# Adding scaled expert outputs to the residual in DRAM by indirect DMA, and SiLU rewritten with Sigmoid and PSUM operands

## The chip, the cores and the metric

The kernel runs on one core of a Trainium2 chip. The metric is the device time of one execution in microseconds (us); the median of three runs of the kernel before is 1481.43 us, the lowest 1478.41 and the highest 1485.65. Five engines work side by side, each through its own list of instructions: TensorE (PE, with its weight loads as PEld), VectorE (DVE), ScalarE (ACT), GpSimd (POOL) and SyncE (SP). They wait for one another through semaphores. DMAs are issued from SP, POOL and ACT.

## The reference, cut to what matters

The input `x` has 4 sequences of 512 tokens with 256 values each, 2048 tokens in all. Two layers each update `x` twice, and every update is multiplied by the tanh of a gate. The second update of each layer is a mixture of eight experts, of which each token uses its best two. Only the mixtures are touched by the change:

```python
# layer 0 (m=0 in the kernel), F = 256; a shared FFN is added as well
p = softmax(h @ w_router.T); top2 of 8 experts, shares renormalised
y = sum over the two experts e of share[e] * (relu(h @ w1[e].T)**2 @ w2[e].T)
x = x + tanh(g_ffn[0]) * (shared(h) + y)
# layer 1 (m=1), F = 512
y = sum over the two experts e of
      share[e] * ((silu(h @ gate_w[e] + gate_b[e]) * (h @ up_w[e] + up_b[e])) @ down_w[e] + down_b[e])
x = x + tanh(g_ffn[1]) * y
```

## The kernel before, in words

All data is float32. A matmul operand is split into a high part (rounded to the type fp32r, which TensorE takes) and a low part (the rest), and `product` (L194 to L196) makes each product of three matmuls. Activations are split by ACT (the rounding copy) and DVE (a subtraction). Expert weights are split on the way in: `weights_hi` (L438) is a casting DMA issued by POOL, and `weights_lo` (L446) is one POOL `tensor_tensor` that subtracts the high part from `raw`, a plain copy of the weights loaded by SP (L376).

The program has five stretches. Part A (attention, shared FFN and the choice of experts of layer 0) lasts until about 386 us of the span. The expert loop of m=0 runs until 521, part C (slot attention with a recurrent update, and the choice of experts of layer 1) until about 1131, the expert loop of m=1 until 1410, and the rest is the combination of m=1. Orders written out by hand set parts A and C; the expert loops are hardware loops.

**Scattering.** When the experts of a batch of 512 tokens are chosen, POOL issues eight indirect DMAs (L759), each of which writes 128 normalised rows of 256 values to their place in the DRAM tensor `routed[m]`, which is sorted by expert. Each expert's rows are filled up with zero rows to groups of G = 256. A table in SBUF holds the first and the last group of each expert. This input gives 19 groups for m=0 and 21 for m=1.

**The loop.** For each expert, each engine runs a hardware loop over its groups. In one turn SP loads the group after the next into `xg` (L387) and stores the result `y` to the DRAM tensor `outputs` (L426). PE multiplies the group with the up weights (in m=1 the gate and the up weights, four parts `f` of 128 columns), turns the rows of the next group (L543), and multiplies with the down weights. For m=0, ACT makes the relu (L475) and its rounded square (L477), DVE makes h in SBUF (L509) and its low part (L521, L524). For m=1, silu(g)·u is computed as (tanh(g/2)+1)·(g/2)·u: ACT writes the tanh (L480) and g/2 (L481) to SBUF, DVE multiplies these two (L513, both inputs in SBUF), then multiplies with the up part in PSUM (L516) and writes h to SBUF; ACT rounds h (L484, L487) and DVE makes the low part from h and the rounded h (L521, L524, both in SBUF). ACT and DVE also split the turned next group (L466, L497). Last, DVE copies the down product out of PSUM (m=0, L529) or adds the bias `DB` (m=1, L531). There is one buffer for `raw`, `xg` and `y`, and two for the split weights of an expert.

**The weights' order.** POOL holds, for each next expert, `weights_hi` and then at once `weights_lo`, without a loop. SP issues the raw weights between the group loops (`raw_in`), and in m=0 at the third expert also five loads of part C's weights (`attention_weights`, L383).

**The combination.** After the loop, POOL waits for the last store and gathers the two rows of each token from `outputs` with 8 indirect DMAs for each batch (L819; 32 for each m), by row numbers `source` that `table_dve` computes. DVE multiplies each with its share and adds it to the residual, 8 instructions a batch (L1257). The residual had been stored to `x_base` and is loaded again. In m=1 SP stores the sum to `out` (L721).

## Time and profile before

| | us |
|---|---|
| median of three runs (lowest, highest) | 1481.43 (1478.41, 1485.65) |
| span of the profiled execution, first to last instruction | 1462.4 |
| its own device time | not recorded beside the span; the three runs lie 16.0 to 23.3 above it |
| PE busy in the span | 1092.1 (75%) |
| DVE / ACT / POOL busy | 790.0 / 418.9 / 362.7 |
| DMA traffic | 114.66 MB, mean 78 GB/s |
| mean granted TensorE clock | 0.872 of full speed |

Stretch by stretch, busy microseconds of each engine:

| stretch of the span | PE | DVE | ACT | POOL | granted clock | DMA share |
|---|---|---|---|---|---|---|
| 402 to 521 (loop of m=0) | 77.97 | 53.45 | 37.49 | 26.46 | 0.89 | 0.61 |
| 521 to 575 (start of part C) | 26.36 | 27.41 | 17.99 | 26.46 | 0.66 | 0.32 |
| 1148 to 1410 (loop of m=1) | 215.51 | 175.75 | 109.89 | 60.53 | 0.91 | 0.40 |
| 1410 to 1462 (combination of m=1) | 0.00 | 13.37 | 0.00 | 31.05 | 0.52 | 0.53 |

A busy share says how full an engine is and not whether it is waited for; the chain of waits says that. Lines are named by number, L513 is line 513 of the kernel before. SPq is SP's queue of DMA issues.

### The profile page before, as it was taken

Reading aid. Unit: us, or ns where it says so; the run is one execution under the profiler, and the core shown is the slowest. Engines: PE = TensorE matmul, PEld = TensorE weight load, DVE = VectorE, ACT = ScalarE, POOL = GpSimd, SP = SyncE. Lnnn points to the kernel's source line nnn. Section 1 sums busy time; section 2 is a strip of 40 time slices with the busy share of each in tenths; the row PEclk is TensorE's granted clock in tenths of the full one; section 3 lists DMA queues with packets and bytes.
Section 4 is the critical chain, followed back from the end, with each engine's and each line's share of the span. In section 5 each row is a group of like instructions: output and inputs, shape, how many; then the busy total and the mean of one; then the engine's idle time right before and its main releaser. Section 6 shows DMA issues by size and latency. Waiting matters only on the chain.

```text
span 1462.4 us, 16573 instructions
## 1 busy us (share of the span) xinstructions
PE 1092.1 (75%) x5562; PEld 904.4 (62%) x5562; DVE 790.0 (54%) x1774; ACT 418.9 (29%) x788; POOL 362.7 (25%) x294
## 2 busy tenths in 40 slices
PE   1978889787666663998999579898971488897850
PEld 1647666575565662786777458686860377897840
DVE  5456546656444436646565544535455466667633
ACT  1203121122132341233332332424220144453420
POOL 4204152131421351410101220101014322213225
PEclk9989989897888985999999679999985599998985
DMA  7600032000375650200000100000005544443435
GB/s 265 225 1 29 1 119 68 1 0 1 132 212 167 179 174 0 58 0 1 1 0 15 44 29 0 1 0 1 1 1 190 176 130 130 130 137 122 129 99 168
DMA packets 92431, 114.66 MB, mean 78 GB/s; under 512 B 6608, under 2 KB 77776, under 8 KB 92240
## 3 DMA queue, kind: packets, MB, share of 16 engines
q1 hardware_dynamic: 72480, 78.46, 16.5%
q0 software_dynamic: 19888, 35.40, 8.3%
q8 instruction: 34, 0.56, 0.2%
q14 instruction: 29, 0.24, 0.1%
HBM read 77.14 MB, written 36.70 MB: 78 GB/s over the span
## 4 chain that ended last, share of the span: by engine, by line
PE 53%; DVE 22%; issue 6%; POOL 6%; ACT 6%; DMA 5%; SPq 2%; DVEq 0%; POOLq 0%; ACTq 0%
PE PS L194 12%; PE PS L196 11%; PE PS L195 11%; PE PS L1577 7%; PE PS L1493 4%; DVE act L513 3%; PE PS L1468 3%; DMA xg<-routed 3%; POOL routed L759 2%; POOL HB L819 2%; POOL rstd L752 2%; PE PS L1389 1%; PE PS L1516 1%; DVE st L1036 1%; DVE SM L1310 1%
## 5 line engine op out<-in xcount | busy, mean ns | idle before, releaser
L752 POOL TENSOR_TENSOR rstd<-ve,minus_half 128x4 f32<-128x4 f32 x40 | 40.6, 1016 | 410.1 <-DVE ve L1043 251.6
L194 PE MATMUL PS<-xt,split 128*128 128x256 f32 x412 | 121.3, 295 | 10.9 <-issue 7.8
L194 PE MATMUL PS<-split,hs 128*128 128x256 f32 x244 | 84.2, 345 | 49.8 <-DVE hs L521 49.8
L195 PE MATMUL PS<-xt,split 128*128 128x256 f32 x412 | 119.3, 290 | 0.0
L196 PE MATMUL PS<-xt,split 128*128 128x256 f32 x412 | 118.9, 289 | 0.0
L1577 PE MATMUL PS<-VP,HB 128*128 128x257 f32 x384 | 97.0, 416 | 16.0 <-DVE VP L1322 16.0
L1577 PEld LDWEIGHTS PS<-VP,HB 128*128 128x128 f32 x384 | 80.1, 210 | 35.2 <-DVE VP L1322 21.8
L513 DVE SCALAR_TENSOR_TENSOR act<-act 128x256 f32<-128x256 f32 x84 | 70.8, 843 | 56.2 <-ACT act L481 56.2
L446 POOL TENSOR_TENSOR split<-raw,split 128x1024 fp32r<-128x1024 f32 (+1 forms) x15 | 66.5, 4432 | 138.4 <-DMA raw<-down_w 81.9
L194 PEld LDWEIGHTS PS<-xt,split 128*128 128x128 f32 x412 | 82.6, 200 | 14.4 <-issue 10.5
L194 PEld LDWEIGHTS PS<-split,hs 128*128 128x128 f32 x244 | 55.9, 229 | 57.1 <-DVE hs L521 57.1
L759 POOL DMA_INDIRECT routed<-S,dest x64 | 65.6, 1024 | 100.2 <-DVE dest L1114 83.0
L195 PEld LDWEIGHTS PS<-xt,split 128*128 128x128 f32 x412 | 82.3, 200 | 0.0
L196 PEld LDWEIGHTS PS<-xt,split 128*128 128x128 f32 x412 | 81.8, 199 | 0.0
L819 POOL DMA_INDIRECT HB<-outputs,source x64 | 63.3, 990 | 73.0 <-DMA outputs<-y 54.2
L195 PE MATMUL PS<-split,hs 128*128 128x256 f32 x244 | 78.1, 320 | 0.0
L196 PE MATMUL PS<-split,hs 128*128 128x256 f32 x244 | 77.8, 319 | 0.0
L543 PE MATMUL PS<-ident,xg 128*128 128x128 f32 x168 | 28.2, 294 | 56.3 <-DMA xg<-routed 56.3
L480 ACT ACTIVATE act<-PS,hbg 128x256 f32<-128x256 f32 x84 | 39.6, 472 | 94.5 <-PE PS L196 94.5
L1389 PE MATMUL PS<-ident,S 128*128 128x128 f32 x208 | 31.1, 299 | 45.1 <-DVE S L1047 45.1
L981 ACT ACTIVATE HB<-PS,SM 128x512 f32<-128x512 f32 x48 | 33.0, 688 | 107.8 <-DVE SM L1312 107.4
L194 PE MATMUL PS<-HTS,WHH 128*128 128x512 f32 x144 | 60.4, 419 | 2.0 <-DVE RT L1051 2.0
(308 smaller groups left out, 2871.4 us busy)
## 6 DMA issues: line engine op xcount, KB each, us to landing
xg<-routed SPq DMA_DIRECT2D x44, 256.0 KB, 2.7
outputs<-y SPq DMA_DIRECT2D x40, 256.0 KB, 3.0
outputs<-zeros SPq DMA_DIRECT2D x3, 2048.0 KB, 16.1
routed<-zeros SPq DMA_DIRECT2D x20, 256.0 KB, 2.5
raw<-m_w SPq DMA_DIRECT2D x16, 256.0 KB, 5.9
split<-m_w POOLq DMA_DIRECT2D x16, 256.0 KB, 4.0
x_base<-X SPq DMA_DIRECT2D x8, 512.0 KB, 3.8
raw<-gate_w SPq DMA_DIRECT2D x8, 512.0 KB, 6.3
```

The lines of the kernel that those rows point to most:

```text
L194: pe.matmul(out_, a[1], b[0], start=first, stop=False)
L195: pe.matmul(out_, a[0], b[1], start=False, stop=False)
L196: return pe.matmul(out_, a[0], b[0], start=False, stop=last)
L446: eng.tensor_tensor(w.split[e % 2][:, 1], w.raw[:], w.split[e % 2][:, 0].bitcast(F32), ALU.subtract).then_inc(sem(f"m{m}_lo"), 1)
L513: dve.scalar_tensor_tensor(out=a[:, 0], in0=a[:, 0], scalar=1.0, in1=a[:, 1], op0=ALU.add, op1=ALU.mult).then_inc(sem(f"m{m}_silu"), 1)
L752: pool.tensor_tensor(rstd[h][:], ve[h][:], minus_half[:], ALU.pow).then_inc(sem("rstd_ready"), 1)
L759: pool.indirect_dma_start(out=routed[m], out_offset=bass.IndirectOffsetOnAxis(ap=dest[m][:, n, j, kk:kk + 1], axis=0), in_=S2[h][:, j], in ...
L819: pool.indirect_dma_start(out=rows_h[h][:, kk, j], out_offset=None, in_=outputs, in_offset=bass.IndirectOffsetOnAxis(ap=source[:, n, j, kk ...
L1389: ins = pe.transpose(bank(h, k + c)[:, j * P:(j + 1) * P], src[:, j, c * P:(c + 1) * P], ident[:])
L1468: ins = pe.matmul(bank(h, b + c), w[:, j, c * P:(c + 1) * P], EWT[:, j], start=j == 0, stop=j == TT - 1)
L1493: ins = pe.matmul(token_banks(h, 0)[:, j], HB[h][:, m, j * P:(j + 1) * P], W2[:, m], start=m == 0, stop=m == HC - 1)
L1577: ins = pe.matmul(bank(h, j)[:, 0:D + 1], HB[h][:, m, j * P:(j + 1) * P], VP[h][:, m, 0:D + 1], start=m == 0, stop=m == TT - 1)
```

## The change

**Rows that know where they belong.** A row of `routed` is four values wider (W = 260): its token number, the share of its second expert, the difference of the first share to that, and the number of its first expert. The choice of experts writes these into `rows_of`, which the eight scattering DMAs send as before. Rows that fill a group (`pad`) carry a token number past the last token and shares of 0.

**The loop.** In each group ACT copies these values to `meta` (`keep`), DVE makes from them each row's share (`row_scale`) and its row number (`row_number`), and ACT writes `y` times the share with two ACTIVATEs (`y_out`; in m=0 straight from PSUM in place of L529, in m=1 after DVE's bias addition). One turn later POOL copies the row numbers and issues two indirect DMAs of 128 rows with addition (`add_rows`). In m=0 one half of a group is added to `x_base[0]` and the other to a second tensor, `x_add`. In m=1 both halves go to `x_base[1]`, and the second half waits until the first has landed. The store of `y`, the tensor `outputs`, its zero fill of three times 2048 KB (now one, for `x_add`), `source` and all 64 gathers are gone.

**The combination.** In m=0 it is one DVE addition of `x_add` for each batch, which is loaded beside the residual. In m=1 there is none: after the last addition SP copies `x_base[1]` to `out` with four DMAs of 512 KB from DRAM to DRAM.

**The split of expert weights.** POOL now runs the group loop too. `weights_hi` of the next expert stands ahead of an expert's loop, `weights_lo` behind its last turn. The load of `raw` moves from SP to ACT's queue at the start of an expert.

**SiLU.** ACT writes a Sigmoid (one ACTIVATE a part in place of two), DVE multiplies it with the biased gate part read from PSUM, then with the up part, and writes h to PSUM; the high and the low part are made from there. In m=0 h is written to PSUM as well. In m=1 the split of the next group now stands ahead of the low part of the last h.

**Starts.** Five of the eight fills of `routed` are issued by ACT, and the first group is loaded after all eight (before: after three). The five loads of part C's weights are issued by SP right at the start of m=0's loop. A few small operations are added to the choice of experts.

```diff
+        sums = [(x_base[0], x_add), (x_base[1], x_base[1])]
...
         def group_in(sp, m, t):
             r = sp.value_load(table[m][0:1, bass.ds(t + 2 * E, 1)], min_val=0, max_val=XROWS - G)
+            if not isinstance(t, int):
+                counted(sp, m)
+                sp.wait_ge(sem(f"m{m}_turned"), t)
+                sp.wait_ge(sem(f"m{m}_kept"), t)
             sp.dma_start(moe[m].xg[:], routed[m][bass.ds(r, G), :].rearrange("(a p) d -> p a d", p=P)).then_inc(sem(f"m{m}_xg"), 16)
...
+        def moe_sp(sp, m):
             sp.wait_ge(sem(f"m{m}_turned"), 1)
+            sp.wait_ge(sem(f"m{m}_kept"), 1)
             group_in(sp, m, 1)
...
+            if m == 0:
+                attention_weights(sp)
+            else:
+                raw_in(sp, 1, 1)
+            total = sp.value_load(table[m][0:1, 2 * E - 1:2 * E], min_val=1, max_val=NG)
+            with sp.Fori(0, total) as t:
+                group_in(sp, m, t + 2)
+            moe_end(sp, m, total)
...
+            def add_rows(t):
+                pool.wait_ge(sem(f"m{m}_next_row"), t + 1)
+                for a in range(2 - m):
+                    pool.wait_ge(sem(f"m{m}_yout{a}"), 16 * (1 + m) * t + 16)
+                pool.sem_inc(sem("passed"), 1)
+                pool.tensor_copy(to_row[:], next_row[:]).then_inc(sem(f"m{m}_to_row"), 1)
+                pool.wait_ge(sem(f"m{m}_to_row"), t + 1)
+                for a in range(G // P):
+                    pool.wait_ge(sem(f"m{m}_y"), 2 * t + 1 + a)
+                    if m == 1 and a == 1:
+                        pool.wait_ge(sem("m1_yout0"), 32 * t + 32)
+                    pool.sem_inc(sem("passed"), 1)
+                    pool.indirect_dma_start(out=sums[m][a], out_offset=bass.IndirectOffsetOnAxis(ap=to_row[:, a:a + 1], axis=0),
+                                            in_=w.y[:, a], in_offset=None, compute_op=ALU.add).then_inc(sem(f"m{m}_yout{a - a * m}"), 16)
+            for a in range(2 - m):
+                pool.dma_start(sums[m][a][B * T:B * T + P], pad[:, 0:D]).then_inc(sem(f"m{m}_yout{a}"), 16)
             pool.wait_ge(sem(f"m{m}_table"), 1)
-            for e in range(2, E):
-                if m == 0 and e == 3:
+            for h in two:
+                pool.wait_ge(sem(f"x_out{h}"), 16 * PAIRS * (m + 1))
+            for e in range(E):
+                if m == 0 and e == 2:
                     attention_weights_hi(pool)
-                weights_hi(pool, m, e)
-                weights_lo(pool, m, e)
+                if 1 <= e < E - 1:
+                    weights_hi(pool, m, e + 1)
+                lo, hi = bounds(pool, m, e)
+                with pool.Fori(lo, hi) as t:
+                    counted(pool, m)
+                    add_rows(t)
+                if 1 <= e < E - 1:
+                    weights_lo(pool, m, e + 1)
+            counted(pool, m)
+            add_rows(hi)
+            moe_end(pool, m, hi)
...
+            def h_hi(t, f):
+                act.wait_ge(sem(f"m{m}_h"), t * w.fc + f + 1)
+                act.activation(w.hs[:, 0, f], h_part(f), ACT.Copy).then_inc(sem(f"m{m}_hhi"), 1)
+            def keep(n):
+                act.wait_ge(sem(f"m{m}_xg"), 16 * n)
+                if not isinstance(n, int):
+                    act.wait_ge(sem(f"m{m}_next_row"), n)
+                    act.wait_ge(sem(f"m{m}_scale"), 2 * n - 2)
+                act.activation(meta[:], w.xg[:, :, D:W], ACT.Copy).then_inc(sem(f"m{m}_kept"), 1)
+            def y_out(t):
+                act.wait_ge(sem(f"m{m}_scale"), 2 * t + 2)
+                if m == 0:
+                    act.wait_ge(sem(f"m{m}_down"), t + 1)
+                else:
+                    act.wait_ge(sem(f"m{m}_biased"), t + 2)
+                for a in range(G // P):
+                    if m == 0:
+                        act.wait_ge(sem(f"m{m}_yout{a}"), 16 * t + 32)
+                    act.activation(w.y[:, a], PS[:, 5 + a, 0:D] if m == 0 else w.y[:, a], ACT.Copy,
+                                   scale=scale[:, a:a + 1]).then_inc(sem(f"m{m}_y"), 1)
...
-                            act.activation(w.act[:, f % 2, 0], PS[:, f, 0:G], ACT.Tanh, bias=hbg[:, b:b + 1], scale=0.5)
-                            act.activation(w.act[:, f % 2, 1], PS[:, f, 0:G], ACT.Identity, bias=hbg[:, b:b + 1], scale=0.5).then_inc(sem(f"m{m}_act"), 1)
+                            act.activation(w.act[:, f % 2, 0], PS[:, f, 0:G], ACT.Sigmoid, bias=col("gate_b", b)).then_inc(sem(f"m{m}_act"), 1)
                             if f:
-                                act.wait_ge(sem(f"m{m}_h"), t * w.fc + f)
-                                act.activation(w.hs[:, 0, f - 1], w.h[:, f - 1], ACT.Copy).then_inc(sem(f"m{m}_hhi"), 1)
-                    if m == 1:
-                        act.wait_ge(sem(f"m{m}_h"), t * w.fc + w.fc)
-                        act.activation(w.hs[:, 0, w.fc - 1], w.h[:, w.fc - 1], ACT.Copy).then_inc(sem(f"m{m}_hhi"), 1)
-                    x_hi(t + 2)
+                                h_hi(t, f - 1)
+                    if m == 0:
+                        keep(t + 2)
+                        x_hi(t + 2)
+                    else:
+                        x_hi(t + 2)
+                        h_hi(t, w.fc - 1)
+                        keep(t + 2)
+                    y_out(t)
...
+            def h_lo(t, f):
+                dve.wait_ge(sem(f"m{m}_h"), t * w.fc + f + 1)
+                dve.wait_ge(sem(f"m{m}_hhi"), t * w.fc + f + 1)
+                dve.tensor_tensor(w.hs[:, 1, f], h_part(f), w.hs[:, 0, f].bitcast(F32), ALU.subtract).then_inc(sem(f"m{m}_hlo"), 1)
+            def row_scale(t, e):
+                dve.wait_ge(sem(f"m{m}_kept"), t + 1)
+                dve.scalar_tensor_tensor(out=here[:], in0=meta[:, :, E0 - D], scalar=float(e), in1=meta[:, :, DSH - D],
+                                         op0=ALU.is_equal, op1=ALU.mult).then_inc(sem(f"m{m}_scale"), 1)
+                dve.wait_ge(sem(f"m{m}_scale"), 2 * t + 1)
+                dve.wait_ge(sem(f"m{m}_y"), 2 * t + 2)
+                dve.tensor_tensor(scale[:], here[:], meta[:, :, SH1 - D], ALU.add).then_inc(sem(f"m{m}_scale"), 1)
+            def row_number(t):
+                dve.wait_ge(sem(f"m{m}_to_row"), t + 1)
+                dve.tensor_copy(next_row[:], meta[:, :, TOK - D]).then_inc(sem(f"m{m}_next_row"), 1)
...
-                            dve.scalar_tensor_tensor(out=a[:, 0], in0=a[:, 0], scalar=1.0, in1=a[:, 1],
-                                                     op0=ALU.add, op1=ALU.mult).then_inc(sem(f"m{m}_silu"), 1)
+                            dve.scalar_tensor_tensor(out=a[:, 1], in0=PS[:, f, 0:G], scalar=col("gate_b", e * w.fc + f),
+                                                     in1=a[:, 0], op0=ALU.add, op1=ALU.mult).then_inc(sem(f"m{m}_silu"), 1)
                             dve.wait_ge(sem(f"m{m}_silu"), t * w.fc + f + 1)
-                            dve.scalar_tensor_tensor(out=w.h[:, f], in0=PS[:, f, G:2 * G], scalar=col("up_b", e * w.fc + f),
-                                                     in1=a[:, 0], op0=ALU.add, op1=ALU.mult).then_inc(sem(f"m{m}_h"), 1)
+                            dve.scalar_tensor_tensor(out=h_part(f), in0=PS[:, f, G:2 * G], scalar=col("up_b", e * w.fc + f),
+                                                     in1=a[:, 1], op0=ALU.add, op1=ALU.mult).then_inc(sem(f"m{m}_h"), 1)
                         if f:
-                            dve.wait_ge(sem(f"m{m}_h"), t * w.fc + f)
-                            dve.wait_ge(sem(f"m{m}_hhi"), t * w.fc + f)
-                            dve.tensor_tensor(w.hs[:, 1, f - 1], w.h[:, f - 1], w.hs[:, 0, f - 1].bitcast(F32), ALU.subtract).then_inc(sem(f"m{m}_hlo"), 1)
-                    dve.wait_ge(sem(f"m{m}_h"), t * w.fc + w.fc)
-                    dve.wait_ge(sem(f"m{m}_hhi"), t * w.fc + w.fc)
-                    dve.tensor_tensor(w.hs[:, 1, w.fc - 1], w.h[:, w.fc - 1], w.hs[:, 0, w.fc - 1].bitcast(F32), ALU.subtract).then_inc(sem(f"m{m}_hlo"), 1)
-                    x_lo(t + 2)
-                    dve.wait_ge(sem(f"m{m}_down"), t + 1)
-                    dve.wait_ge(sem(f"m{m}_yout"), 16 * t + 1)
+                            h_lo(t, f - 1)
                     if m == 0:
-                        dve.tensor_copy(w.y[:], PS[:, 5:7, 0:D]).then_inc(sem(f"m{m}_y"), 1)
+                        h_lo(t, w.fc - 1)
+                        x_lo(t + 2)
                     else:
+                        x_lo(t + 2)
+                        h_lo(t, w.fc - 1)
+                        row_number(t)
+                        dve.wait_ge(sem(f"m{m}_down"), t + 1)
+                        dve.wait_ge(sem(f"m{m}_yout0"), 32 * t + 48)
                         dve.tensor_tensor(w.y[:], PS[:, 5:7, 0:D], DB[:, e].unsqueeze(1).to_broadcast([P, G // P, D]),
-                                          ALU.add).then_inc(sem(f"m{m}_y"), 1)
+                                          ALU.add).then_inc(sem(f"m{m}_biased"), 1)
...
-            def combine(m, n, h):
-                x_t = residual(n, h) if m == 0 else X[h]
...
+            def combine(n, h):
+                if n < 2:
+                    dve.wait_ge(sem(f"x_in{h}"), 16 * (PAIRS + 2))
                 else:
-                    dve.wait_ge(sem(f"x_in{h}"), 16 * (PAIRS + 1) + (m and 16 * (n // 2 + 1)))
...
-                    for j in range(TT):
-                        ins = dve.scalar_tensor_tensor(out=x_t[:, j], in0=rows_h[h][:, kk, j], scalar=share[m][:, n, j, kk:kk + 1],
-                                                       in1=x_t[:, j], op0=ALU.mult, op1=ALU.add)
...
+                    dve.wait_ge(sem(f"second_in{h}"), 48)
+                x_t = residual(n, h)
+                dve.tensor_tensor(x_t[:], x_t[:], added[n], ALU.add).then_inc(sem("combined"), 1)
...
+            for n in range(B):
+                sp.dma_start(out[n], x_base[1][n * T:(n + 1) * T]).then_inc(sem(f"x_out{n % 2}"), 16)
```

On POOL, in the loop of m=1, this stood for one next expert (L438 `weights_hi`, L446 `weights_lo`, L434 reads the table):

```order
L434 TENSOR_LOAD table
L434 ISA x2
L438 DMA split<-gate_w 128x2x512
L438 DMA split<-up_w 128x2x512
L438 DMA split<-down_w 128x4x256
L446 TENSOR_TENSOR split<-raw,split 128x3072
```

and this stands there now for one expert (L442 and L450 are the two halves of the split, L466 and L473 are `add_rows`):

```order
L487 UNCONDITIONAL_BRANCH
L462 REGISTER_ALU
L464 ISA
L466 COPY to_row<-next_row 128x2
L469 ISA
L473 DMA x_base<-y,to_row 2176x256
L469 REGISTER_ALU
L471 REGISTER_ALU
L473 DMA x_base<-y,to_row 2176x256
L487 REGISTER_ALU
L487 COMPARE_AND_BRANCH
L450 TENSOR_TENSOR split<-raw,split 128x3072
```

The subtraction moved behind the additions of the expert's last group turn, and each turn holds two DMAs that were not on POOL.

On DVE, the end of one turn of the loop of m=1 was this (parts 2 and 3 of h, then the split of the next group and the bias):

```order
L505 REGISTER_ALU
L513 SCALAR_TENSOR_TENSOR act<-act 128x256
L516 SCALAR_TENSOR_TENSOR h<-PS,colv,act 128x256
L521 TENSOR_TENSOR hs<-h,hs 128x256
L524 TENSOR_TENSOR hs<-h,hs 128x256
L496 REGISTER_ALU
L497 TENSOR_TENSOR xt<-PS,xt 128x512
L526 REGISTER_ALU
L527 ISA
L531 TENSOR_TENSOR y<-PS,DB 128x512
```

and is now this (L603 and L606 are the two multiplications, L569 the low part of h, L562 that of the next group, L583 `row_number`):

```order
L595 REGISTER_ALU
L603 SCALAR_TENSOR_TENSOR act<-PS,colv,act 128x256
L606 SCALAR_TENSOR_TENSOR PS<-PS,colv,act 128x256
L569 TENSOR_TENSOR hs<-PS,hs 128x256
L561 REGISTER_ALU
L562 TENSOR_TENSOR xt<-PS,xt 128x512
L569 TENSOR_TENSOR hs<-PS,hs 128x256
L583 CAST next_row<-meta 128x2
L618 ISA
L619 TENSOR_TENSOR y<-PS,DB 128x512
```

Every large operation now names PS among its inputs, the split of the next group stands one place earlier, and the row numbers stand ahead of the bias.

On SP, between and in the group loops of m=0, this stood (L376 raw weights, L387 the next group; the store of y, L426, follows):

```order
L376 DMA raw<-m_w 128x2x256 x2
L354 TENSOR_LOAD table
L354 ISA x2
L355 TENSOR_LOAD table
L355 ISA x2
L420 UNCONDITIONAL_BRANCH
L422 REGISTER_ALU
L386 ISA
L386 TENSOR_LOAD table
L386 ISA x2
L387 ISA
L387 DMA xg<-routed 128x2x256
```

and this stands there now:

```order
L429 UNCONDITIONAL_BRANCH
L429 ISA
L399 TENSOR_LOAD table
L399 ISA x2
L402 REGISTER_ALU
L404 ISA
L404 DMA xg<-routed 128x2x260
L429 REGISTER_ALU
L429 COMPARE_AND_BRANCH
```

The raw weights no longer stand ahead of a group's load, and no store of y follows it.

## Rows read from the trace of the kernel before

**Rows 1.** Page, the chain that ended last: shares of the span by engine.

```profile
PE 53%; DVE 22%; issue 6%; POOL 6%; ACT 6%; DMA 5%; SPq 2%; DVEq 0%; POOLq 0%; ACTq 0%
```

**Rows 2.** Chain of waits in m=1's loop: start us, us, what.

```profile
1159.53 6.39 DVE hs L521
...
1194.43 6.90 DVE act L513
...
1366.20 5.99 DVE act L513
```

**Rows 3.** Groups by line, 1150 to 1410: count, busy us, mean ns, idle us.

```profile
L513 DVE SCALAR_TENSOR_TENSOR act<-act 128x256 f32<-128x256 f32 x84 | 70.8, 843 | 56.2 <-ACT act L481 56.2
L484 ACT ACTIVATE hs<-h 128x256 fp32r<-128x256 f32 x63 | 26.2, 416 | 32.9 <-DVE h L516 32.6
```

**Rows 4.** Timeline, POOL and DVE, m=1: start us, us, instruction, [idle before].

```profile
1158.69 6.93 POOL L446 TENSOR_TENSOR split<-raw,split 128x3072 fp32r<-128x3072 f32 x1 [17.94 <-DMA raw<-down_w]
1159.13 0.48 DVE L516 SCALAR_TENSOR_TENSOR h<-PS,colv,act 128x256 f32<-128x256 f32 x1
1194.34 6.70 POOL L446 TENSOR_TENSOR split<-raw,split 128x3072 fp32r<-128x3072 f32 x1 [11.71 <-DMA raw<-down_w]
```

**Rows 5.** SP's timeline in m=1: stores of y, the first, three, the last.

```profile
1171.24 0.39 SPq L426 DMA_DIRECT2D outputs<-y  x1
...
1191.71 0.39 SPq L426 DMA_DIRECT2D outputs<-y  x1
...
1208.77 0.39 SPq L426 DMA_DIRECT2D outputs<-y  x1
...
1218.44 0.39 SPq L426 DMA_DIRECT2D outputs<-y  x1
...
1409.59 0.39 SPq L426 DMA_DIRECT2D outputs<-y  x1
```

**Rows 6.** Timelines of DVE and POOL in the tail.

```profile
1408.63 0.69 DVE L531 TENSOR_TENSOR y<-PS,DB 128x512 f32<-128x512 f32 x1 [0.56 <-PE PS L196]
1412.68 1.04 POOL L819 DMA_INDIRECT HB<-outputs,source  x1 [40.77 <-DMA outputs<-y]
...
1452.22 0.95 POOL L819 DMA_INDIRECT HB<-outputs,source  x1 [0.30 <-issue]
```

**Rows 7.** DMA issues: count, KB each, median us from issue to landing.

```profile
outputs<-zeros SPq DMA_DIRECT2D x3, 2048.0 KB, 16.1
...
out<-X SPq DMA_DIRECT2D x4, 512.0 KB, 3.3
...
routed<-S,dest POOLq DMA_INDIRECT x64, 2.4
HB<-outputs,source POOLq DMA_INDIRECT x64, 2.8
```

**Rows 8.** The gathers' line L819: us from issue to landing.

```profile
DMA to landing us min/median/max: 2.6/2.8/6.8
```

**Rows 9.** SP's timeline, m=0.

```profile
410.32 0.40 SPq L426 DMA_DIRECT2D outputs<-y  x1
...
475.86 1.00 SPq L376 DMA_DIRECT2D raw<-m_w  x2
479.30 0.38 SPq L387 DMA_DIRECT2D xg<-routed  x1
...
516.19 0.39 SPq L426 DMA_DIRECT2D outputs<-y  x1
...
520.58 0.39 SPq L426 DMA_DIRECT2D outputs<-y  x1
```

**Rows 10.** PE's transposes of xg in m=0, 405 to 521: idle us, times.

```profile
  DMA xg<-routed: 25.6, 8
```

**Rows 11.** DVE's timeline at the start of part C.

```profile
544.72 8.06 DVE L1291 TENSOR_TENSOR KK<-S,KK 128x1024 fp32r<-128x1024 f32 x1 [4.42 <-ACT KK L963]
552.70 3.37 DVE L1257 SCALAR_TENSOR_TENSOR X<-HB,share,X 128x256 f32<-128x256 f32 x8
```

232 lines of the change are left out of this document (94 added, 138 removed), and 4 rows, old and new, of the table ORDER_C.

## The prediction, made before the changed kernel was run

> **What bounds the kernel now.** I began with the page's chain that ended last: 53% of it is PE and 22% DVE [rows 1]. So the kernel is not bound by DMA or POOL as a whole, and an edit pays only where the chain leaves PE. The chain read in order of time shows two such places that this change touches. In the loop of m=1 single DVE operations of 6 to 7 us stand in the chain; there are seven, one on L521 and six on L513 [rows 2]. All 84 of L513 take 70.8 us; without the six, at 6.3, 33 are left for 78, 0.42 each [rows 3]. The timeline shows why: POOL's split of an expert's weights, L446, starts at 1194.34 and lasts 6.70 us, and the long L513 starts at 1194.43 and ends with it [rows 2, 4]. L513 and L521 read two tiles in SBUF. An operation that reads one from PSUM is not stretched: L516 began at 1159.13, inside the split that began at 1158.69, and took its usual 0.48 [rows 4].
>
> What a split costs a group is read from SP's stores of y. Without one they are 9.67 us apart (1208.77 to 1218.44), with one 17.06 (1191.71 to 1208.77). From the first to the last store 20 intervals take 238.35 us [rows 5]. Twenty of 9.67 are 193.4, so 45 is over. About 1 us at each of six steps into a new expert stays (an estimate: the seven long operations lie between 5.9 and 6.9, less 0.42, so the six splits in these intervals make 36 to 39). I put the six at 39. The seventh falls in group 0 and costs up to 6.0 ahead of the first store.
>
> The other place is the tail. The last bias addition ends at 1409.32 and the span at 1462.4, 53.1 us later; 32 gathers of about 1.28 us fill 40 of these, one behind another [rows 6].
>
> **Durations that the trace lacks.** No DMA with addition is in it. I call L the time from its issue to its landing, for 128 rows of 1 KB. The indirect write of 128 such rows has a median of 2.4, the indirect read 2.8 [rows 7], the read's worst is 6.8 [rows 8]. An addition has to read and to write, so I take 3.6 (2.4 with 1.2 for the reading, half of 2.4), with the ends 2.4 and 6.8. The Trainium skill, "DMA: Bandwidth & Descriptors", fits a DMA issued by GpSimd with 2.0 us and bytes over 436 GB/s, which would be 2.3 for 128 KB, close to the 2.4 of [rows 7]. With L = 2.3 the sum below would be some 22 us lower; that is a rival further down.
>
> The four copies from DRAM to DRAM are not in it either. Stores of 512 KB take 3.3 each, so 13 in a row; the three zero fills have a median of 16.1, in which 4 MB were written, so 8 for 2 MB [rows 7]. A copy reads as well: 16 and 2 to land make the upper end. I take 12, between 8 and 18.
>
> **Tail: 53.1 before.** Now: the first half of `y_out` 0.42 (as L484, [rows 3]) and 0.3 for POOL to start; the first addition 3.6, the second, which waits for it, 3.6 and 0.1; the wait's release and SP's issues 0.8; the copies 12. Sum 20.8, gain 32. Ends: 8 and L = 2.4 give 14.4 (gain 39), 18 and L = 6.8 give 33.2 (gain 20).
>
> **Loop of m=1.** Two things happen to the six splits. The stretched DVE operations go, since L603, L606 and L569 each read PSUM, as L516 did unhindered [rows 4]. But the split now stands behind the additions of the expert's last turn. What stands behind the waiting POOL instruction is the split itself, and PE waits for it before the next expert. Count from the end of a down product: 0.56 and 0.69 to the end of the bias [rows 6], 0.42 for `y_out`, 0.1, L = 3.6, 1.04 for the second issue [rows 6], 6.7 for the split [rows 4], 0.3 to PE: 13.4. The group's own work is 9.7, so PE waits 3.7 at each of six experts, 22 us. Before it was 39: gain 17. Group 0 is relieved of up to 6.0; against it stands loading ACT's table for the Sigmoid, which I put at 2, for a gain of 4. Small operations are added: per group `keep`, `row_scale`, `row_number` and two ACTIVATEs, about 1.5 us over ACT and DVE. ACT and DVE are idle at the start of a group (L513 waited 56.2 us in all for ACT, which waited for PE, [rows 3]), so I put them at 0.2 a group, 4 us. The Sigmoid form saves an ACTIVATE in each part, which shortens the last part's path by about 0.4 a group, at most 8; cover for it is PE's transposes and the first three down weights, so I take nothing. Together gain 17. Ends: L = 2.4 and all of the 8, gain 33; the whole gain of the splits lost, 0.
>
> The buffer y is a loop of its own now: bias 0.69, `y_out` 0.42, 0.3, two additions one behind another 2L. That is 1.4 + 2L = 8.6 at L = 3.6, just under 9.67. It takes over from L = 4.15.
>
> The port rule bears on `row_scale` (two small SBUF inputs) and `row_number` (a copy). The Trainium skill, "SBUF — State Buffer", section "Who interferes with whom", says that such operations contend with GpSimd and that the second one waits until the first is done; the 6.90 of [rows 2] agrees for two inputs, and no row has such a copy. By it `row_number` would hold the bias of the expert's last group until the split ends. At L = 3.6 this costs nothing, as PE waits for the same split; at L = 5 it would add about 2 us at each of six experts.
>
> **Loop of m=0.** The stores of 19 groups go from 410.32 to 520.58: 18 intervals of 6.13 on average; an undisturbed one is 4.39 (516.19 to 520.58) [rows 9]. PE waits 25.6 us for xg in 8 cases [rows 10], and the order shows one reason: two loads of raw weights stand ahead of the group's load, which follows 3.4 us later (475.86, 479.30 [rows 9]). With raw on ACT's queue I let 16 of the 25.6 go. Against it, POOL's turn is a loop: both additions landed, copy of the numbers 0.4, first issue and gap 1.35, second addition L: 1.75 + L = 5.35. That is over 4.39, by 0.96 in about ten undisturbed turns: 10 lost. Net gain 6. The five loads of part C's weights are now early, beside the first groups; that I leave in the range. Ends: gain 18 (L = 2.4, no turn held), loss 15 at L = 4.5.
>
> **Start of part C.** L1291 took 8.06 at 544.72, beside POOL's weight subtractions. Scaled from L1257 (3.37 for 8 times 256 columns [rows 11]) its 1024 columns are worth 1.7. Without gathers these subtractions run some 20 us earlier, when DVE waits for PE: gain 6.4. The combination of batches 0 and 1 is one addition of 1024 columns each, 1.7 for 3.37: gain 3.4. Instead of a store's 3.0 the last group needs `y_out`, two issues and L, about 5.6: loss 2.5. The extra loads of `x_add` lie beside other loads. With 1 us for the later batches the gain is 8; ends 12 and, if the loads are late by one of 512 KB, 3.
>
> **Starts of the loops.** All eight fills come before the first group's load, but five go through another queue: loss 2 in m=0, gain 2 in m=1. The additions to the choice of experts lose 1.
>
> **Sum.** −32 −17 −6 −8 +1 = −62. The span would be 1400.4. The median of the runs is 19.0 over the profiled span of 1462.4 and I carry that over: 1419.4, which I round to 1420.
>
> **Rivals.** (A) The split gives back all that the ports gave. For this the split's late place, and ACT, which issues the raw loads only when the weights before are split, speak: the split of a two-group expert may then find its raw weights not landed. At 6.5 a step in place of 3.7 the gain of 17 is gone: 1437. Against it, raw is asked for a whole expert ahead. (B) The slower side: a slow adding DMA. Place: y's loop in m=1 (1.4 + 2L) and POOL's in m=0 (1.75 + L). At L = 5: m=1, 14 turns by 1.7 and six splits at 5.1, +16 in place of −17; m=0 +12; tail −29; part C −7; starts +1: −7. It decides from L = 5.3, where nothing is gained. At 6.8, the worst gather [rows 8]: m=1 +76, m=0 +46, tail −26, part C −5, +1: +92, 1573. For it: addition reads before it writes, and raw loads of 0.5 MB each share the queues. Against it: all medians of indirect DMAs lie below 3. (C) DVE is held in spite of its PSUM operands: each split costs 6 as before and group 0 is not relieved, 1441. [Rows 4] speak against it. (D) L is 2.4, as the plain scatter: tail −2.4, splits −7, m=0 −10, part C −1 more: 1400. (E) Copies from DRAM to DRAM take 40 rather than 12, by queues that nothing in this trace fills so: 1448.
>
> **Chances.** Forecast 0.50, A 0.17, B 0.10, C 0.03, D 0.15, E 0.05. A measurement of this kernel tells 0.5%, 7.4 us, from no change. B's lower part falls within that and a little of it under, so: faster 0.85, within 0.06, slower 0.09. The range of 1390 to 1464 takes in the forecast with its ends, A, C, D and E, and leaves B out.
>
> **What would show it.** In the profile after: no DVE operation of 6 us in m=1's chain, POOL's split late in an expert's last group, and PE idle behind it for about 3.7; adding DMAs landing in 3 to 4.5; group turns of 9.7 in m=1 and about 5.5 in m=0; some 21 us from the last bias to the end; the start of part C without an 8 us operation. The prediction is wrong if L is over 4.2, if the copies take over 18, or if PE waits at the splits as long as before.

## The result, and the profile after

The changed kernel is slower: 1525.68 us (median of 4 runs, 1522.63 to 1528.41) against 1480.66 us of the kernel before (4 runs, 1478.41 to 1485.65). The ratio is 1.031, with a 95% interval of 1.0274 to 1.0346. The forecast was 1420.

In the page of the kernel after, these lines answer to [rows 1] (busy microseconds and share of each engine, then the chain that ended last):

```profile
span 1525.5 us, 17240 instructions
...
PE 1118.9 (73%) x5562; PEld 923.2 (61%) x5562; DVE 780.6 (51%) x1833; ACT 429.1 (28%) x827; POOL 442.9 (29%) x363
...
DMA 12%; issue 5%; POOL 2%; PE 1%; POOLq 1%; ACT 1%; DVE 0%; ACTq 0%; SPq 0%; DVEq 0%
DMA x_base<-y,to_row 11%; POOL split L450 1%; POOL split L442 1%; DMA raw<-down_w 0%; ACT y L525 0%; PE PS L204 0%; DMA routed<-pad 0%; PE PS L206 0%; PE PS L205 0%; ACTq L408 0%; POOLq L363 0%; DMA xg<-routed 0%; POOL x_base L473 0%; POOLq
```

The chain's shares add up to little here, as it could be followed only through part of the span; what it names is the adding DMAs with 11%, and no DVE operation.

The stretches say where the time went. The borders are the first transposes of `xg` in each loop, the first matmul of part C, and the start of the first and the end of the last bias addition in m=1. The kernel before is given twice, from the trace of the prediction and from a second one (`before_again`, below):

| stretch, us | before | before, second | after |
|---|---|---|---|
| up to m=0's first transposes | 396.0 | 401.1 | 404.7 |
| loop of m=0 | 126.9 | 129.5 | 166.5 |
| part C and the start of m=1 | 625.2 | 634.1 | 618.3 |
| m=1 up to the first bias | 22.3 | 22.5 | 30.4 |
| m=1 from there to the last bias | 239.0 | 239.5 | 286.0 |
| tail | 53.1 | 53.1 | 19.6 |
| span | 1462.4 | 1479.8 | 1525.5 |

The execution of the second trace took 1481.54 us, 1.7 more than its span; that of the trace after 1527.25, 1.75 more. So the 19.0 us that the prediction put around the span were not there: the runs that have both numbers have them 1.5 to 1.8 apart, so its trace must have been of a short execution (on another chip the kernel before went down to 1459.59). The difference of the medians, 45 us, is to be compared with the second column. The two loops lost 37 and 54 (the second with its start up to the first bias), the tail and part C gave 33.5 and 16.

The mean granted clock of the loops fell as well: from 0.83 to 0.77 in m=0's and from 0.93 to 0.86 between m=1's first and last bias, where PE's busy time rose from 200.2 to 208.3 us. In m=1 that is not what holds the turns. Of the 21 bias additions 13 waited for the landing of an addition and only two for PE (the other six stand behind a held operation, shown below):

```profile
  DMA x_base<-y,to_row: 61.8, 13
  PE PS L206: 3.3, 2
```

In m=0 no run tells the clock's share from the rest.

POOL's timeline of m=1 in the kernel after (start, length, instruction, idle time before and its releaser) answers to [rows 4]:

```profile
1244.78 1.59 POOL L473 DMA_INDIRECT x_base<-y,to_row  x1 [7.81 <-DMA x_base<-y,to_row]
1248.67 0.19 POOL L466 COPY to_row<-next_row 128x2 int32<-128x2 int32 x1 [2.30 <-DMA x_base<-y,to_row]
1250.63 1.56 POOL L473 DMA_INDIRECT x_base<-y,to_row  x1 [1.77 <-ACT y L525]
1255.15 1.53 POOL L473 DMA_INDIRECT x_base<-y,to_row  x1 [2.96 <-DMA x_base<-y,to_row]
1259.09 0.19 POOL L466 COPY to_row<-next_row 128x2 int32<-128x2 int32 x1 [2.41 <-DMA x_base<-y,to_row]
1261.05 1.56 POOL L473 DMA_INDIRECT x_base<-y,to_row  x1 [1.77 <-ACT y L525]
1265.86 1.54 POOL L473 DMA_INDIRECT x_base<-y,to_row  x1 [3.26 <-issue]
1266.87 7.23 POOL L450 TENSOR_TENSOR split<-raw,split 128x3072 fp32r<-128x3072 f32 x1
1273.48 1.38 POOL L442 DMA_DIRECT2D split<-gate_w  x1
...
1277.62 1.71 POOL L473 DMA_INDIRECT x_base<-y,to_row  x1 [1.03 <-issue]
1288.62 1.60 POOL L473 DMA_INDIRECT x_base<-y,to_row  x1 [9.29 <-DMA x_base<-y,to_row]
```

An ordinary turn goes from 1250.63 to 1261.05, 10.4 us: the first addition until the second may start 4.52, the second until the copy 3.94, then 1.96 for bias, `y_out` and POOL. An expert's last turn has the split behind both additions, from 1266.87 to 1274.10. And the first addition in the next expert's first turn needs 11.00 until the second may start (1277.62 to 1288.62), not 4.52: at that moment the casts (L442) and the raw weights are on their way.

DVE's bias additions show the three kinds of turns, and one operation that should not be there:

```profile
1219.87 0.69 DVE L619 TENSOR_TENSOR y<-PS,DB 128x512 f32<-128x512 f32 x1 [9.18 <-DMA x_base<-y,to_row]
...
1248.54 0.69 DVE L619 TENSOR_TENSOR y<-PS,DB 128x512 f32<-128x512 f32 x1 [7.22 <-DMA x_base<-y,to_row]
...
1258.96 0.69 DVE L619 TENSOR_TENSOR y<-PS,DB 128x512 f32<-128x512 f32 x1 [2.60 <-DMA x_base<-y,to_row]
...
1266.86 7.37 DVE L583 CAST next_row<-meta 128x2 int32<-128x2 f32 x1
1274.04 0.68 DVE L619 TENSOR_TENSOR y<-PS,DB 128x512 f32<-128x512 f32 x1
...
1292.17 0.69 DVE L619 TENSOR_TENSOR y<-PS,DB 128x512 f32<-128x512 f32 x1 [6.32 <-DMA x_base<-y,to_row]
```

From the second row on the turns end 10.4, 15.1 and 18.1 us apart. Over the whole loop, six last turns average 15.0, six first turns 17.9 and the other eight 11.0; together 285.3. The cast of two numbers a partition, usually 0.16 us, lasts 7.37 beside the split. Six of them do, between 7.25 and 7.79, one beside each of the six splits.

The adding DMAs themselves, by their line (duration on POOL, then landing, min/median/max):

```profile
L473 POOL DMA_INDIRECT x_base<-y,to_row x64: 1532/1558/1708, 410.4 to 1511.8; - x64
L473 POOL DMA_INDIRECT x_add<-y,to_row x20: 1533/1558/1604, 412.4 to 567.3; - x20
...
DMA to landing us min/median/max: 3.5/3.9/10.6
```

The median landing is 3.9, where 3.6 was taken. The issue takes 1.56 us of POOL; the plain ones of [rows 6] took 0.95 to 1.04.

POOL in the loop of m=0, one turn:

```profile
487.00 0.19 POOL L466 COPY to_row<-next_row 128x2 int32<-128x2 int32 x1 [2.78 <-DMA x_add<-y,to_row]
488.06 1.56 POOL L473 DMA_INDIRECT x_base<-y,to_row  x1 [0.87 <-ACT y L525]
489.93 1.55 POOL L473 DMA_INDIRECT x_add<-y,to_row  x1 [0.30 <-issue]
493.89 0.19 POOL L466 COPY to_row<-next_row 128x2 int32<-128x2 int32 x1 [2.42 <-DMA x_add<-y,to_row]
```

It is closed in itself: copy, 0.87 idle until `y_out` is done, issue, issue, landing, 6.89 us from copy to copy, where an undisturbed turn of PE took 4.39 [rows 9]. This is the shortest: the 19 steps from copy to copy in this loop go up to 11.3 and average 8.2.

Two places came out as forecast. The tail (ACT's, POOL's and SP's timelines) answers to [rows 6]; from the end of the last bias, 1505.85, to the end of the span it is 19.65:

```profile
1505.94 0.91 ACT L525 ACTIVATE y<-y,scale 128x256 f32<-128x256 f32 x2 [2.43 <-DVE y L619]
...
1507.23 1.56 POOL L473 DMA_INDIRECT x_base<-y,to_row  x1 [1.75 <-ACT y L525]
1511.76 1.55 POOL L473 DMA_INDIRECT x_base<-y,to_row  x1 [2.97 <-DMA x_base<-y,to_row]
...
1515.38 2.52 SPq L795 DMA_DIRECT2D out<-x_base  x4
```

And DVE at the start of part C answers to [rows 11]: the 8 us operation is 1.23, the combination 1.22.

```profile
594.41 1.23 DVE L1339 TENSOR_TENSOR KK<-S,KK 128x1024 fp32r<-128x1024 f32 x1 [4.45 <-ACT KK L1016]
595.56 1.22 DVE L1311 TENSOR_TENSOR X<-X,HB 128x1024 f32<-128x1024 f32 x1
```

### The profile page after: what moved, and what is told of

The parts are those of the page before. It is cut to its first block and busy times, and to the rows that moved or that the text cites. A ratio compares the mean times of both kernels' runs of the same rounds, so it can differ in the third digit from the quotient of the medians.

```text
span 1525.5 us, 17240 instructions
## 1 busy us (share of the span) xinstructions
PE 1118.9 (73%) x5562; PEld 923.2 (61%) x5562; DVE 780.6 (51%) x1833; ACT 429.1 (28%) x827; POOL 442.9 (29%) x363
## 5 line engine op out<-in xcount | busy, mean ns | idle before, releaser
L204 PE MATMUL PS<-xt,split 128*128 128x256 f32 x412 | 128.4, 312 | 71.9 <-issue 69.1
L473 POOL DMA_INDIRECT x_base<-y,to_row x64 | 101.6, 1587 | 153.3 <-DMA x_base<-y,to_row 94.1
L204 PEld LDWEIGHTS PS<-xt,split 128*128 128x128 f32 x412 | 89.0, 216 | 75.5 <-issue 71.9
L205 PE MATMUL PS<-xt,split 128*128 128x256 f32 x412 | 125.8, 305 | 0.0
L206 PE MATMUL PS<-xt,split 128*128 128x256 f32 x412 | 125.5, 305 | 0.0
L1622 PE MATMUL PS<-VP,HB 128*128 128x257 f32 x384 | 100.4, 427 | 15.6 <-DVE VP L1370 15.6
L205 PEld LDWEIGHTS PS<-xt,split 128*128 128x128 f32 x412 | 89.2, 217 | 0.0
L206 PEld LDWEIGHTS PS<-xt,split 128*128 128x128 f32 x412 | 88.7, 215 | 0.0
L450 POOL TENSOR_TENSOR split<-raw,split 128x1024 fp32r<-128x1024 f32 (+1 forms) x15 | 72.5, 4833 | 28.6 <-DMA raw<-down_w 19.3
L204 PE MATMUL PS<-RT,W 128*128 128x512 f32 x96 | 42.1, 439 | 25.8 <-DVE RT L1271 17.6
L603 DVE SCALAR_TENSOR_TENSOR act<-PS,colv,act 128x256 f32<-128x256 f32 x84 | 40.3, 480 | 35.9 <-ACT act L543 31.4
```

What stands on the lines that cost most here:

```text
L204: pe.matmul(out_, a[1], b[0], start=first, stop=False)
L205: pe.matmul(out_, a[0], b[1], start=False, stop=False)
L206: return pe.matmul(out_, a[0], b[0], start=False, stop=last)
L450: eng.tensor_tensor(w.split[e % 2][:, 1], w.raw[:], w.split[e % 2][:, 0].bitcast(F32), ALU.subtract).then_inc(sem(f"m{m}_lo"), 1)
L473: pool.indirect_dma_start(out=sums[m][a], out_offset=bass.IndirectOffsetOnAxis(ap=to_row[:, a:a + 1], axis=0), in_=w.y[:, a], in_offset=No ...
L603: dve.scalar_tensor_tensor(out=a[:, 1], in0=PS[:, f, 0:G], scalar=col("gate_b", e * w.fc + f), in1=a[:, 0], op0=ALU.add, op1=ALU.mult).the ...
```

## The experiments

The runs were made on several chips; each ratio is to runs of the kernel before on the same chip. For an edit of the changed kernel the distance of its ratio from 1.031 is what the edit is worth; 0.01 of it is 14.8 us. The same kernel, the rewrite alone, gave 0.9623 on one chip and 0.9688 on another, so between chips a distance under about 0.007 says nothing.

**A control.** The kernel before once more.

> The kernel before, unchanged, for a second trace, so that the stretches of its first trace can be told from the scatter between executions. The first trace had 396.0 us to the first transposes, 126.9 for m=0's loop, 625.2 to m=1's first transposes, 22.3 to the first bias, 239.0 to the end of the last, 53.1 for the tail. Expected: every stretch within 1.5% of these, the first one within 10 us (the traces of the other kernels, which leave part A nearly alone, lie between 397.9 and 405.1).

All stretches of the loops and the tail repeat within about 2% (m=0's loop by 2.0%, over the 1.5% expected); part C was 9 us longer, 1.4%, and the first stretch 5. So of the stretches, 5 to 9 us in the long ones are scatter between executions, and the loops' 37 and 54 are not.

**The other half of the change alone.**

```diff
-  act.activation(w.act[:, f % 2, 0], PS[:, f, 0:G], ACT.Tanh, bias=hbg[:, b:b + 1], scale=0.5)
-  act.activation(w.act[:, f % 2, 1], PS[:, f, 0:G], ACT.Identity, bias=hbg[:, b:b + 1], scale=0.5)
+  act.activation(w.act[:, f % 2, 0], PS[:, f, 0:G], ACT.Sigmoid, bias=col("gate_b", b))
...
-  dve.scalar_tensor_tensor(out=w.h[:, f], in0=PS[:, f, G:2 * G], ..., in1=a[:, 0])
+  dve.scalar_tensor_tensor(out=PS[:, f, G:2 * G], in0=PS[:, f, G:2 * G], ..., in1=a[:, 1])
```

> The kernel before with only the other half of the change: Sigmoid in place of tanh and g/2, every large DVE operation of both expert loops reading PSUM, h in PSUM, the split of the next group one place earlier in m=1. Stores, gathers, POOL's order and all DMAs as before. Theory (the stretched DVE operations were held by POOL's weight split because both inputs lay in SBUF): the six 6 us excesses and the one in group 0 go, about 39 + 6 us, so 1480 becomes about 1436 (1425 to 1446), and no DVE operation of m=1's loop lasts over 1 us. Rival (POOL's split holds DVE whatever it reads, or PE would then wait for the weights themselves at the same point): within 10 us of 1480.

Ratio 0.9623 (0.9589 to 0.9657), 1418.03 us against 1470.63; on another chip 0.9688 (0.9658 to 0.9717), 1433.24 against 1479.30. The gain of 2.8 to 4.1% takes in the 3.0% first expected, though on the first chip alone it is more; on the second, where I had expected 0.962 again, it is less. The first trace shows why. DVE's groups between 1155 and 1380 (count, busy us, mean ns, idle us) answer to [rows 3], POOL's split to [rows 4]:

```profile
L526 DVE SCALAR_TENSOR_TENSOR PS<-PS,colv,act 128x256 f32<-128x256 f32 x84 | 41.4, 493 | 3.0
L523 DVE SCALAR_TENSOR_TENSOR act<-PS,colv,act 128x256 f32<-128x256 f32 x84 | 40.7, 485 | 52.9 <-ACT act L487 48.6
L508 DVE TENSOR_TENSOR hs<-PS,hs 128x256 fp32r<-128x256 f32 x84 | 34.9, 415 | 0.0
```

```profile
1195.34 6.81 POOL L448 TENSOR_TENSOR split<-raw,split 128x3072 fp32r<-128x3072 f32 x1 [10.84 <-DMA raw<-down_w]
```

The split lasts 6.81 as before, and beside it no operation is stretched: the means are the usual durations. Turns in m=1 are 9.6, 10.6 into a new expert, one of 15.0. From m=1's first transposes to the last bias it takes 219.6 us (261.3 before). So the changed kernel threw away a good half: this half is worth about 43 us in m=1, some 7 of them up to the first bias (15.2 for 22.3).

**No additions in a loop.** `add_rows` copies its numbers and waits for y, but issues no DMA; waits for landings are gone.

```diff
+  if m != 1:        # noadd_m0: if m != 0
       pool.indirect_dma_start(out=sums[m][a], ..., compute_op=ALU.add)
```

> The changed kernel without m=1's adding DMAs and their waits (expert outputs of layer 1 are left out; 21 groups as before). Theory (of the 55 us that m=1's loop lost, the additions' landings make nearly all, POOL's late split the small rest): ordinary turns 9.6, last turns of an expert up to 11.5; the loop's 21 bias additions span 225 us in place of 285, the tail is 8 shorter: ratio to before 0.985 (0.975 to 0.995). Rival (the split's late place costs most of it, as it did before the rewrite, 6 us at each of six experts): span of 250 or more, ratio 1.005 or more.

> The changed kernel without m=0's 38 adding DMAs and their waits (expert outputs of layer 0 are left out, so later values and the number of groups in m=1 may differ; only the stretch up to part C is read). Copies, waits for y and POOL's splits stay. Theory (m=0's loop is bound by POOL's turn of 6.9 us, copy, two issues of 1.56 and a landing): the loop from its first transposes to part C's first matmul falls from 166 us to 118 (110 to 126), below the 127 of before. Rival (the split behind the expert's last turn or the raw weights on ACT's queue set it): it stays above 145.

noadd_m1: 0.9683 (0.9643 to 0.9723), beyond the expectation. The bias additions span 204.4 us, not 225: even turns with a split are 9.4 or 9.5, and steps into a new expert 10.9; only around one expert of two groups are they 10.9 and then 12.7. POOL shows why I was wrong on the rest:

```profile
1234.85 0.19 POOL L466 COPY to_row<-next_row 128x2 int32<-128x2 int32 x1 [9.30 <-DVE next_row L584]
1237.73 6.82 POOL L450 TENSOR_TENSOR split<-raw,split 128x3072 fp32r<-128x3072 f32 x1 [2.69 <-ACT y L526]
```

Without landings ahead of it the split begins 2.9 us after the copy and is over before PE has finished the turn. Its late place costs next to nothing alone. m=1 from its first transposes to the last bias is 226.5 us here and 316.4 in the changed kernel: 90 us hang on the additions. noadd_m0 (one execution, no interval): m=0's loop 124.2, within the expectation, against 166.5: 42 us hang on the additions there. It is still 8 to 10 us longer than in the last experiment below, which has no additions either; what these are is taken up at the end.

**What of an adding DMA costs.** The same DMAs without the addition:

```diff
-  in_=w.y[:, a], in_offset=None, compute_op=ALU.add)
+  in_=w.y[:, a], in_offset=None)
```

> The changed kernel with plain indirect writes in place of the adding ones, at the same places with the same waits (the rows overwrite the residual, so the sum is left out). Theory (the queue and the turn of waits matter, but the addition has a price too: its issue takes 1.56 us against 1.0 and lands 3.8 after issue against 2.4): m=0's turn falls from 6.9 to about 5.0, 19 of them, -30 us; m=1's two halves in a row fall by 2 x 1.4, of which ordinary turns can use 0.8 (14 of them, -10) and first turns 2 to 3 (-15): about 1472 (1460 to 1490). Rival (an adding DMA is as cheap as a plain one, and what is slow is any indirect DMA in this place): within 8 us of 1526.

0.989 (0.9853 to 0.9927), 0.042 lower and within the expectation, though some 10 us of it are a group less in m=1 (the other residual sends rows elsewhere; 20 groups). The stretch that has its 19 groups either way is m=0's loop: 166.5 to 143.0, 23.5 less where I had expected 30. The issue took 0.97 us and landed after 2.5 (median) in place of 1.56 and 3.9. So of m=0's 42 us, 23.5 are the addition, the rest that two indirect DMAs and a landing stand in every turn.

**The second half waiting for the first.**

```diff
-  sums = [(x_base[0], x_add), (x_base[1], x_base[1])]
+  sums = [(x_base[0], x_add), (x_base[1], x_add)]
...
-  if m == 1 and a == 1:
-      pool.wait_ge(sem("m1_yout0"), 32 * t + 32)
```

> The changed kernel with m=1's two halves added to two tensors, as in m=0, so that the second does not wait for the first (the second tensor is not added to the output, so half of the expert outputs is left out). Theory (m=1's y goes round in 0.7 + 0.5 + 0.8 + 2 x 4.2 us = 10.4, over PE's 9.7): ordinary turns fall to 9.7 (8 of them, -6 us), first turns of an expert by 2 to 3 us since only one landing stands behind the queue (-15), the last turns by nothing: about 1505 (1495 to 1515). Rival (the serial halves cost nothing beside the weights): within 5 us of 1526.

1.0036 (1.001 to 1.0062): 0.027 lower, 40 us where 21 were expected. Ordinary turns are 9.5, as expected nearly; but last turns, for which I had expected nothing, fell from 15.0 to 12.3, since the split starts 2.7 us earlier after the bias, and first turns from 17.9 to 14.2. This kernel leaves half of m=1's expert outputs out of the result. Both halves in one tensor at once wasn't tried: nothing but the data would keep two additions off the same row.

**What slows an expert's first addition.** I read it as the queue: the casts stand ahead of the additions on POOL. Five kernels on that.

```diff
+  if e >= 2:        # hi_small: the casts; raw_small: the raw loads; raw_hi_small: both
+      dst, ap = dst[:, :, 0:16], ap[:, :, 0:16]
```

```diff
-  if 1 <= e < E - 1: weights_hi(pool, m, e + 1)
   lo, hi = bounds(pool, m, e)      # hi_late, par_hi_late
+  if 1 <= e < E - 1: add_rows(lo); weights_hi(pool, m, e + 1); lo = lo + 1
```

> The changed kernel, in which the casting DMAs of weights_hi bring only 16 columns of each block from expert 2 on (the rest of the high parts is left as it was, so the products are of other weights; instructions, waits and counts are the same). Theory (in the first turn of an expert the adding DMAs stand behind 1.5 MB of casting DMAs in POOL's one queue; they land in 9.5 to 11.4 us there against 4.5 elsewhere): first turns of 17.2 to 18.9 us in m=1 fall by 5 to 7 each, six of them, 36 us, and m=0 gives 5 to 15: 1526 becomes about 1480 (1470 to 1492). Rival (the addition itself or POOL's late split sets these turns): within 8 us of 1526.

> The changed kernel with weights_hi of the next expert issued behind the additions of an expert's first group turn instead of ahead of them. Nothing is left out. Theory (the six first turns of an expert in m=1 are long because the adding DMAs queue behind the casting DMAs): as with the short casts, which gave 1.3% and first turns of 14.3 in place of 17.9 us, so ratio to the kernel before 1.018 (1.012 to 1.024). Rival (the short casts helped because 9 MB fewer crossed the DMA engines, not because of the queue's order): ratio stays at 1.031 within 0.004.

> The kernel with m=1's halves in two tensors (the second not added to the output) and weights_hi behind the first turn's additions. With halves in parallel the ratio was 1.0036. Theory: first turns fall from 13.9 to about 11, six of them, so 17 us, ratio 0.992 (0.987 to 0.997). Rival (with only one landing in a row nothing waits for the queue any more): ratio 1.0036 within 0.003.

> The changed kernel in which the loads of the raw weights bring only 16 columns of each block from expert 2 on (the low parts are then of other weights); casts, order and waits as changed. Theory (the first additions of an expert are slowed by the raw weights on ACT's queue as much as by the casts ahead of them): from the first addition's issue to the second's 6 to 7.5 us in place of 10.4, ratio 1.012 to 1.020. Rival (only what stands ahead in POOL's own queue slows them): 9 us or more, ratio over 1.024.

> The changed kernel with both the raw loads and the casts at 16 columns from expert 2 on. Theory (the two transfers are the whole reason): the first addition of an expert takes 4.6 to 5 us to the second's issue, like any other, first turns 12.0 to 13.0 (the split still stands ahead of them), ratio 1.000 to 1.010. Rival (something else in the first turn, POOL's issue of the casts or the split): over 6 us.

| kernel | ratio (95%) | six first additions, until the second may start, mean us |
|---|---|---|
| changed | 1.031 (1.0274 to 1.0346) | 10.4 |
| hi_late | 1.0169 (1.0131 to 1.0208) | 8.1 |
| hi_small | 1.0184 (1.0143 to 1.0226) | 6.9 |
| raw_small | 1.0051 (1.0024 to 1.0079) | 6.9 |
| raw_hi_small | 1.0013 (0.9994 to 1.0033) | 4.7 |
| par_hi_late | 0.992 (0.9892 to 0.9948) | (halves in parallel) |

The expectations missed here are of hi_small, where 1526 was to become 1480 and the ratio stayed at 1.018 (first turns fell from 17.9 to 14.7, not by 5 to 7), and of raw_small's ratio. par_hi_late came out at its ratio by luck: first turns were 13.3 and not 11, and of the 18 us between its trace and m1_parallel's only 3.3 lie between m=1's first and last bias, while m=0's loop gave 7.6 and part C 6.

The ratio of hi_late came out as expected, and yet the theory behind it was half wrong. In its trace the casts are issued after both additions, and the first still takes 8.87 us:

```profile
1261.25 1.56 POOL L473 DMA_INDIRECT x_base<-y,to_row  x1 [1.54 <-ACT y L528]
1270.12 1.56 POOL L473 DMA_INDIRECT x_base<-y,to_row  x1 [7.30 <-DMA x_base<-y,to_row]
```

With both transfers short it takes what any other takes:

```profile
1266.61 1.71 POOL L479 DMA_INDIRECT x_base<-y,to_row  x1 [1.03 <-issue]
1271.31 1.60 POOL L479 DMA_INDIRECT x_base<-y,to_row  x1 [2.99 <-DMA x_base<-y,to_row]
```

So the raw weights, which another engine issues on another queue, slow the addition by 3.5 us (10.4 to 6.9), about as much as the casts in its own queue. The landings show it too: the slowed addition lands with the last of the raw weights, at 1287.8 and 1287.6 in the changed kernel, at 1269.3 and 1269.2 in hi_late. The Trainium skill, "DMA: Bandwidth & Descriptors", section "Issuing engines are not separate DMA queues", says that all of them run on the same 16 DMA engines and interleave; these runs agree. raw_small and raw_hi_small had 20 groups in m=1, so about 10 us (0.007) of their ratios isn't from the transfers; the last column is free of that.

**The split and the held cast.**

```diff
+  n = w.cols if e < 2 else 16
-  eng.tensor_tensor(w.split[e % 2][:, 1], w.raw[:], ...)
+  eng.tensor_tensor(w.split[e % 2][:, 1, 0:n], w.raw[:, 0:n], ...)
```

> The changed kernel with POOL's subtraction weights_lo on 16 columns from expert 2 on (the low parts of the other columns are left as they were); everything else as changed. Theory (the split stands behind two landings of about 4.5 us, so in an expert's last turn PE waits for it, and the next expert's first additions start behind it): last turns fall from 15.0 to 10.4, first turns from 17.9 to about 15, six each, and m=0 gives about 5 x 1.5: about 52 us less, ratio 0.996 (0.990 to 1.004). Rival (the additions alone set these turns, and the split lies under them): 1.031 to 1.020.

> The changed kernel with m=1's row numbers (the cast L583, which waited 7.37 us beside POOL's split) ahead of the second part of h, as in m=0, so that it runs before the split. Nothing is left out. Theory (PE waits for the same split anyway, and the next additions stand behind it on POOL): no gain, ratio 1.031 within 0.004, though no cast lasts over 1 us any more. Rival (the held cast delays the bias and with it y and the additions): first turns of an expert shorter by 2 to 5 us, ratio 1.010 to 1.022.

lo_small: 0.9988 (0.9962 to 1.0014). In company with the additions the split does cost: m=1 from the first bias to the last is 245.2 us for 286.0, m=0's loop 160.1 for 166.5. It stands between two landings and PE. row_early (L583 moved ahead of h's second part): 1.0257 (1.0214 to 1.03), between the two expectations and not clearly apart from the changed kernel. Its line shows the cast freed:

```profile
L583 DVE CAST next_row<-meta x40: 157/160/333, 408.6 to 1493.0; 128x2 int32<-128x2 f32 x40
```

Last turns fall to about 11.1, and the first turns behind a split rise to between 20.2 and 21.7, if the weights are asked for in them too, and to 18.1 if not: POOL's next addition still stands behind the split. The stretch to the last bias is 283.4 for 286.0. The held cast shows a stall of 7.37 us and costs at most a few in all.

**The raw weights on ACT's queue, without additions.** The rewrite alone, and `raw_in` moved from SP to ACT:

```diff
-  raw_in(sp, m, e + 1)
+  raw_in(act, m, e + 1)
```

> The kernel before with the SiLU and PSUM rewrite (ratio 0.962), and the raw weights issued from ACT's queue at an expert's start, as in the change, in both loops. The forecast gave this edit 16 us in m=0, since PE waited 25.6 us for xg behind raw loads on SP. Theory after the trace without m=0's additions (its loop took 124.2 us with this edit in it, 126.9 before): the edit is worth 0 to 3 us, so ratio 0.962 within 0.004. Rival (the 16 us are there and were hidden by POOL's longer turn): m=0's loop under 115 us, ratio 0.952 or less.

> The SiLU and PSUM rewrite alone once more, beside the next kernel on the same chip: ratio 0.962 (0.958 to 0.966).

> The rewrite with the raw weights on ACT's queue once more. Theory (m=0's loop gained 13 us in the trace, 116.0 against 128.9): ratio 0.954 (0.950 to 0.958), below the rewrite alone by more than the intervals. Rival (the gain of the loop was of that one execution, or is given back in part C, whose stretch was 634 against 623 there): the two within 0.003 of each other.

0.9596 (0.9565 to 0.9627), and on the second chip 0.9591 (0.9555 to 0.9628) against 0.9688 (0.9658 to 0.9717) for the rewrite alone. I had expected the ratio of the rewrite alone in the first of these runs, and the ratio fell within that; about the loop the rival, under 115 us, was nearly right. In the second run the ratio was to be 0.950 to 0.958 and just missed it. m=0's loop is 116.0 and 114.0 us against 128.9 and 129.3, and in m=1 the one turn of 15.0 (13.7 in the second trace) is gone: before it the split waited for the raw weights, and now the six splits of the loop wait for their casts. On that chip the two kernels differ by 1%, their intervals don't touch; in the first pair they overlap. This is the fastest version found: 1417.32 us against 1479.30 before, with nothing left out.

## Why the prediction was wrong

**Tail** (gain 32): right, 33.5. The copies took 10.1, of the 12 taken.

**Start of part C** (gain 8): right in kind. Operations of 1.23 and 1.22 us where 8.06 and 3.37 stood. The stretch gave 6.9 against the first trace and 15.8 against the second; the part above 8 isn't to be told from scatter between two traces. Over all traces the stretch took 623 to 634 us in the six of the kernel before and its edits and 612 to 619 in the twelve of the changed kernel and its edits; the means are 12 apart.

**Loop of m=1** (gain 17): this failed, by 71 us (54 lost). The part on the ports was right: alone it gives about 43, and the forecast had 39 and, for group 0, 4. It then took 22 back for the split's late place. What failed is the step "The buffer y is a loop of its own now ... just under 9.67". Its form was right, its terms too small: 10.4 in place of 8.6, and so over 9.67. The two landings made 0.4 of the 1.8 (about 3.8 each in these turns, for 3.6). The rest is hand-overs: POOL began 0.8 after `y_out` and not 0.3, the second issue stood 0.8 behind the first's landing, which had no term in this sum (0.1 in the tail's), and `y_out` took 0.1 more and began 0.1 later. The rival that ended on the other side named this place and set the turning point of the whole at L = 5.3; with the terms as measured it was passed at 3.9.

Worse, the loop was priced by its ordinary turns. The last turn of an expert was to be 13.4 and was 15.0. The first turn had no term of its own beyond the 1 us of a new expert, although all of the next expert's weights, 3 MB, are asked for in it. Against the rewrite alone (203.7 us from the first bias to the last, 285.3 here) six first turns of 17.9 for 11.4 (10.6 and one of 15.0) make 39, six last turns of 15.0 for 9.6 make 32, and the other eight 10. lo_small shows that the late split, which alone cost next to nothing, makes 41 of these in company with the additions. What did hold is the forecast's remark that a held `row_number` costs little where PE waits for the same split.

**Group 0** (gain 4): wrong sign, 8.1 lost in the first trace. The split of expert 1 stands ahead of all additions, and the first bias waits for an addition of nothing (9.18 us, in the first row of the biases above). Without the additions the stretch is 21.4, with the rewrite alone 15.2.

**Loop of m=0** (gain 6): failed, 37 to 40 lost. POOL's turn was put at 5.35 and is 6.9 at its shortest: 0.7 more from the copy to the first issue (1.06 for 0.4), 0.5 more from issue to issue (1.87 for 1.35), 0.4 for the landing (3.96 for 3.6). And it was let lengthen ten undisturbed turns only, by 0.96 each, with the long ones left as they were. But POOL's turns average 8.2: the additions of this loop land after 3.7 to 5.0 us, beside weights after up to 8.7, and the casts and splits stand between them. The 16 us for xg were there (13 to 15 in the last experiment) but hidden behind POOL's turn.

Not all of this loss is additions: without them the loop took 124.2, and with the rewrite and the raw weights on ACT's queue 116.0 and 114.0. One difference is in the order of DVE's work. It makes h only after `row_scale`, which waits for `y_out` of the group before, and that waits for the down product. In noadd_m0 this wait and then PE's for the low part of h are

```profile
L579 DVE TENSOR_TENSOR scale<-here,meta 128x2 f32<-128x2 f32 x18 | 2.9, 162 | 28.3 <-ACT y L526 28.3
...
  PE PS L204: 28.6, 16
```

and in silu_raw_act, which has no `row_scale`, PE's is

```profile
  PE PS L194: 4.1, 7
```

The forecast had a term for the small operations in m=1 (0.2 us a group) and none in m=0. No run changes their order, so it is argued and not shown that the 8 to 10 us come from it.

**Starts**: the first stretch was 404.7 against 396.0 and 401.1; traces of kernels that leave it alone lie between 397.9 and 405.1, so nothing can be read from it.

**The conversion**: the 19.0 us around the span rested on a trace of one short execution. It moved the forecast's baseline, not its sign.

The chances were wrong in one way above all: slower had 0.09, because the rival was tied to one unknown, L, when its place depended as much on small hand-overs. Of one of them the trace of before had the size: its last store of y lands at 1411.81, and POOL's first gather, which waits for it, starts at 1412.68 [rows 6], 0.87 later, where the forecast put 0.1 between the landing of one addition and the issue of the next in the tail, and nothing in the ring. Why POOL began 0.8 after `y_out` and not 0.3 stays open.

## What to carry to other kernels

A result handed on by a read-modify-write makes a closed ring of engines (bias, scaling, issue, landing, copy). Add up its ring with every hand-over, and work it out for each kind of turn, the ordinary one, the one with a split and the one in which weights are loaded. And two edits in one change are to be timed apart: here one alone gave 3 to 4%, and both together lost 3%.

## What was not expected of the hardware

An indirect DMA with addition occupies POOL for 1.56 us and lands after 3.9, against 0.97 and 2.5 for the same DMA without. Beside the next expert's 3 MB of weights, half of them in its own queue and half in another, it takes 10.4 until the next may start, and 6.9 beside either half. POOL's next issue stands 0.8 behind the landing that it waits for. And a DVE cast of 128 x 2 numbers waited 7.37 us for a POOL `tensor_tensor`: the Trainium skill, "SBUF — State Buffer", section "Who interferes with whom", has it so for copies and casts, and row_early, where it ran ahead of the split, had none over 0.33.
